# Attention scores from 64-row halves: one score product per head, a mask added by VectorE, and a new order of the steps

## The reference

```python
q, k = (rope(q), rope(k))
scores = jnp.einsum('bqhd,bkhd->bhqk', q, k) / math.sqrt(hd)
scores = jnp.where(causal, scores, jnp.asarray(-1000000000.0, scores.dtype))
probs = jax.nn.softmax(scores, axis=-1)
attn = jnp.einsum('bhqk,bkhd->bqhd', probs, v).reshape(Bb, Tt, d) @ Wproj
```

## Time and profile before

| | us |
|---|---|
| median of 3 runs | 1647.37 (1645.69 to 1647.99) |
| the profiled execution, own time | 1637.57 |
| its span, first to last instruction | 1635.7 |
| TensorE busy | 1437.9 (88%) |
| VectorE busy | 1033.1 (63%) |
| ScalarE busy | 912.9 (56%) |
| GpSimd busy | 717.7 (44%) |

### The profile page before, as it was taken

The page is one execution under the profiler, slowest core; times in us unless marked ns, Lnnn a source line. Parts: engine busy times, 40 slices in busy tenths (PEclk is TensorE's granted clock), DMA queues, the critical chain, the costliest instruction groups (busy, mean ns, idle before and its releaser), DMA issues.

```text
span 1635.7 us, 27557 instructions
## 1 busy us (share of the span) xinstructions
PE 1437.9 (88%) x9777; PEld 1248.5 (76%) x9777; DVE 1033.1 (63%) x2453; ACT 912.9 (56%) x2160; POOL 717.7 (44%) x712
## 2 busy tenths in 40 slices
PE   7988699999999997589869898889865999999996
PEld 5767599999999986466747666667654999999996
DVE  2998367766776757466756776768554555655552
ACT  5876255555555532267756676758744545554552
POOL 0787443344334114433453545644334444544443
PEclk9998799999999998799988998989876999999998
DMA  5410356555655531676575675676533223433312
GB/s 179 136 56 31 84 164 182 154 163 174 180 155 163 147 112 43 111 125 123 115 131 110 112 136 101 114 126 110 94 129 100 73 55 90 97 90 88 52 22 26
DMA packets 139448, 182.00 MB, mean 111 GB/s; under 512 B 22485, under 2 KB 107296, under 8 KB 139312
## 3 DMA queue, kind: packets, MB, share of 16 engines
q1 hardware_dynamic: 110512, 127.23, 31.3%
q0 software_dynamic: 28160, 51.96, 16.0%
q10 hardware_dynamic: 640, 1.05, 0.4%
HBM read 107.28 MB, written 42.08 MB: 91 GB/s over the span
## 4 chain that ended last, share of the span: by engine, by line
PE 67%; DVE 13%; issue 7%; another core or an unknown queue 7%; ACT 3%; POOL 2%; DMA 1%; SPq 1%; ACTq 0%; DVEq 0%; POOLq 0%
PE banks L942 41%; PE banks L1473 4%; PE banks L1430 4%; PE banks L451 3%; PE banks L1526 2%; PE banks L1004 2%; DVE hidden L977 2%; PE banks L1486 2%; PE banks L1447 1%; DVE lo_w L911 1%; DVE rm L1727 1%; DVE X L1695 1%; PE banks L1540 1%; DVE smax L1685 1%
## 5 line engine op out<-in xcount | busy, mean ns | idle before, releaser
L942 PE MATMUL banks<-hi_x,hi_w 128*128 128x320 f32 (+1 forms) x832 | 293.6, 353 | 35.0 <-DVE hidden L977 24.8
L942 PE MATMUL banks<-lo_x,hi_w 128*128 128x320 f32 (+1 forms) x832 | 288.5, 347 | 0.0
L942 PE MATMUL banks<-hi_x,lo_w 128*128 128x320 f32 (+1 forms) x832 | 288.2, 346 | 0.0
L942 PE MATMUL banks<-hi_w,hi_h 128*128 128x256 f32 x896 | 261.4, 292 | 5.9 <-issue 3.5
L884 POOL DMA_INDIRECT xe<-pooled,idx x160 | 155.5, 972 | 228.3 <-PE banks L1004 183.3
L942 PE MATMUL banks<-lo_w,hi_h 128*128 128x256 f32 x896 | 254.1, 284 | 0.0
L942 PE MATMUL banks<-hi_w,lo_h 128*128 128x256 f32 x896 | 254.0, 284 | 0.0
L942 PEld LDWEIGHTS banks<-hi_x,hi_w 128*128 128x128 f32 x832 | 160.2, 192 | 57.8 <-DVE hidden L977 29.7
L1878 POOL DMA_INDIRECT out<-X,tab x64 | 106.7, 1667 | 200.5 <-DVE X L1978 185.9
L1579 ACT ACTIVATE PN<-banks,smax 128x256 f32<-128x256 f32 (+1 forms) x512 | 180.2, 442 | 14.8 <-DVE smax L1685 13.8
L942 PEld LDWEIGHTS banks<-hi_w,hi_h 128*128 128x128 f32 x896 | 171.9, 192 | 7.6 <-issue 5.1
(11 more groups left out here) (186 smaller groups left out, 3101.0 us busy)
## 6 DMA issues: line engine op xcount, KB each, us to landing
w<-in_L_ffn_w SPq DMA_DIRECT2D x96, 256.0 KB, 5.6
done<-res SPq DMA_DIRECT2D x32, 640.0 KB
QS<-parts_qk SPq DMA_DIRECT2D x128, 128.0 KB
BIG<-in_L_ffn_W SPq DMA_DIRECT2D x16, 1024.0 KB
KS<-parts_qk SPq DMA_DIRECT2D x120, 128.0 KB
mask<-in_c_masks SPq DMA_DIRECT2D x16, 257.0 KB, 2.8
pooled<-XF SPq DMA_DIRECT2D x16, 256.0 KB, 3.3
WS<-in_L_cond_W SPq DMA_DIRECT2D x16, 256.0 KB
```

The source lines that it names most:

```text
L942: last = e.matmul(o, a[i], b[j], start=start and k == 0, stop=stop and k == 2, skip_group_check=True)
```

## The change

The block of zeros goes: `KS` keeps the two heads of a pair on rows 0 to 63 and 64 to 127, without the other halves, and GpSimd's memsets go. Scores are made for one head at a time, from 64 rows. Part 0 of a group is now the second query tile of all four heads: four products of 256 columns, head halves in turn, the halves in banks 0 and 1. Parts 1 and 2 are the first query tile of one half each: a mask product of 256 columns and two products of 128, both in bank 2; part 2 waits for part 1's semaphore. The mask of the second tile is no longer a product: VectorE adds it, while it takes the row minimum of the negated sum and writes that sum to `PN`, and ScalarE takes the exponentials there in place. The next group's part 0 waits for VectorE's row maxima instead of ScalarE's exponentials. The eight table entries of a routing group are issued four in each of two items. The five tables are new, and the number of instructions in a round differs only by these parts.

```diff
-    KS1 = sb("KS1", [P, HQ, NPAIR, T], F32R, place)
+    KS1 = sb("KS1", [P, NPAIR, T], F32R, place)
...
-    tri_q = np.where(p[None, :] > p[:, None], -1e9, 0.0)
+    tri_q = np.concatenate([np.zeros((P, P)), np.where(p[None, :] > p[:, None], -1e9, 0.0)], 1)
...
     PE_ROUND = (
-        ("rank", -3), ("scores", -1, 3, 0), ("turn_p", -1, 2, 2), ("scores", -1, 3, 1), ("values", -1, 1),
...
+        ("norm_turn", 1), ("scores", -1, 3, 1), ("turn_p", -1, 2, 2), ("turn_p", -1, 2, 0), ("scores", -1, 3, 2),
...
+    def entry_at(b, i):
+
+        if group_ended(b) is not None:
+            return group_ended(b), i
+        return (group_ended(b - 1), TB * K1 + i) if group_ended(b - 1) is not None else None
...
     def stack(e, b, x):
         e.wait_ge(s_qk_lo, 2 * b + x + 1)
-        if b < 2 and x == 1:
-            e.wait_ge(s_blocks, b + 1)
...
-                dst = KS[b % 2][rows_, s, :, :] if x else QS[b % 2][rows_, :, :]
+                dst = (KS if x else QS)[b % 2][rows_, :, :]
...
     def pe_scores(e, G, part):
-        if G >= 1:
-            e.wait_ge(s_pn, exp_count(G - 1, part))
-        if part < 2:
-            pair = 2 * g + part
-            e.matmul(PS[:, part, :].rearrange("p (h a k) -> p h a k", h=HQ, a=2)[:, :, 1, :], ident_b[:, :],
-                     wide(causal[:, :], 1, [P, HQ, P]), start=True, stop=False, skip_group_check=True)
-            last = e.matmul(PS[:, part, :], QS[b % 2][:, pair, P:T], KS[b % 2][:, :, pair, :],
-                            start=False, stop=True, skip_group_check=True)
+        half = lambda t, s: t[b % 2][s * P // HQ:(s + 1) * P // HQ]
+        if part == 0:
+
+            if G >= 1:
+                e.wait_ge(s_smax, 5 * (G - 1) + 4)
+            for x in range(2):
+                for s in range(HQ):
+                    last = e.matmul(PS[:, s, x * T:(x + 1) * T], half(QS, s)[:, 2 * g + x, P:T], half(KS, s)[:, 2 * g + x, :],
+                                    start=True, stop=True, skip_group_check=True)
+                    if x == 1:
+                        last.then_inc(s_s[s], 1)
         else:
-            e.matmul(PS[:, 2, :].rearrange("p (h k) -> p h k", h=HG), ident_b[:, :], wide(causal[:, :], 1, [P, HG, P]),
-                     start=True, stop=False, skip_group_check=True)
+
+            s = part - 1
+            if s == 1:
+                e.wait_ge(s_s[2], 2 * G + 1)
+            elif G >= 1:
+                e.wait_ge(s_pn, exp_count(G - 1, 2))
+            e.matmul(PS[:, 2, s * T:(s + 1) * T].rearrange("p (h k) -> p h k", h=2), ident_b[:, :],
+                     wide(causal[:, :], 1, [P, 2, P]), start=True, stop=False, skip_group_check=True)
             for x in range(2):
-                pair = 2 * g + x
-                last = e.matmul(PS[:, 2, x * T:(x + 1) * T], QS[b % 2][:, pair, 0:P], KS[b % 2][:, :, pair, 0:P],
-                                start=False, stop=True, skip_group_check=True)
-        last.then_inc(s_s[part], 1)
+                last = e.matmul(PS[:, 2, (2 * s + x) * P:(2 * s + x + 1) * P], half(QS, s)[:, 2 * g + x, 0:P],
+                                half(KS, s)[:, 2 * g + x, 0:P], start=False, stop=True, skip_group_check=True)
+            last.then_inc(s_s[2], 1)
...
             elif step == "row_max":
-                e.tensor_reduce(smax[:, G % NPN, col:col + heads_], PS[:, part, :].rearrange("p (x k) -> p x k", x=heads_),
-                                AX.X, ALU.max, negate=True).then_inc(s_smax, 1)
+                if part < 2:
+
+                    for x in range(2):
+                        cols, col = slice(x * T, (x + 1) * T), 2 * part + x
+                        e.tensor_tensor_reduce(PN[:, slot, part, cols], PS[:, part, cols], masks[:, :], -1.0, 3.0e38,
+                                               ALU.add, ALU.min, smax[:, slot, col:col + 1]).then_inc(s_smax, 1)
+                else:
+                    e.tensor_reduce(smax[:, slot, HG:2 * HG], PS[:, 2, :].rearrange("p (x k) -> p x k", x=HG),
+                                    AX.X, ALU.max, negate=True).then_inc(s_smax, 1)
```

More of the change, by code:

```diff
@@ L1177, in _build @@
[L1177 to L1180, removed]
-    DVE_ROUND = (
[L1182 to L1188, removed]
@@ new lines, in _build @@
+        ("qk", 1, 0), ("qk", 1, 1), ("values", -1, 1), ("turn_p", -1, 2, 1), ("gate_turn", -2),
+        ("turn_p", -1, 3, 2), ("turn_p", -1, 3, 0), ("values", -1, 2), ("rank", -3), ("turn_p", -1, 3, 1),
+        ("turn_qk", 1, 0), ("scores", 0, 0, 0), ("scores", 0, 0, 1), ("values", -1, 3), ("x_turn", 2),
+        ("scores", 0, 0, 2), ("gate", -2), ("scores", 0, 1, 0), ("outputs", -1, 0), ("turn_p", 0, 0, 2),
+        ("outputs", -1, 1), ("turn_p", 0, 0, 0), ("turn_qk", 1, 1), ("scores", 0, 1, 1), ("out_turn", -1),
@@ new lines, in _build @@
+        ("scores", 0, 1, 2), ("turn_p", 0, 0, 1), ("scores", 0, 2, 0), ("proj", -1), ("matrix", 2),
+        ("turn_p", 0, 1, 2), ("scores", 0, 2, 1), ("turn_p", 0, 1, 0), ("scores", 0, 2, 2), ("scores", 0, 3, 0),
+        ("values", 0, 0), ("turn_p", 0, 1, 1), ("v", 1))
+    DVE_ROUND = (
+        ("row_max", -1, 2, 0), ("row_max", -1, 2, 1), ("proj", -2), ("norm", -2, 1), ("matrix", 1),
+        ("norm", 1, 0), ("row_max", -1, 2, 2), ("route", -3, 1), ("scale", 1, 0), ("row_max", -1, 3, 0),
+        ("row_max", -1, 3, 1), ("combine", 2, 0), ("row_max", -1, 3, 2), ("scale", -2, 1), ("qk", 1, 0),
+        ("qk", 1, 1), ("route", -3, 2), ("route", -3, 3), ("combine", 2, 1), ("place", -3), ("row_max", 0, 0, 0),
+        ("split", 1, 0), ("row_max", 0, 0, 1), ("row_max", 0, 0, 2), ("gate", -2), ("row_max", 0, 1, 0),
+        ("outputs", -1, 0), ("outputs", -1, 1), ("row_max", 0, 1, 1), ("route_shift", -2), ("split", 1, 1),
+        ("row_max", 0, 1, 2))
@@ L1207, in _build @@
     PE_LAST = (
[L1208 removed]
+        ("turn_p", 15, 2, 2), ("scores", 15, 3, 1), ("values", 15, 1), ("turn_p", 15, 2, 0),
         ("turn_p", 15, 2, 1), ("gate_turn", 14), ("scores", 15, 3, 2), ("values", 15, 2), ("gate", 14),
@@ L1390, in pool_attn @@
         for step, b, d in rounds(POOL_FIRST, POOL_ROUND, POOL_LAST):
-            if step == "blocks" and b == 0:
-                e.memset(KS0[:, :, :, :].bitcast(F32), 0.0).then_inc(s_blocks, 1)
-            elif step == "blocks":
-                pool_zero_blocks(e)
-            elif step == "got":
+            if step == "got":
                 t, k = d
@@ L1413, in pool_attn @@
                                 ALU.add).then_inc(s_base, 1)
-            elif step == "entry" and group_ended(b) is not None:
-                g = group_ended(b)
-                t0 = r1.tiles(g)[0]
+            elif step == "entry" and entry_at(b, d[0]):
+                g, i = entry_at(b, d[0])
+                tt, k = r1.tiles(g)[0] + i // K1, i % K1
                 if d[0] == 0:
```

93 lines of the change are left out of this document (46 added, 47 removed).

## The result

| | before | after |
|---|---|---|
| median of 4 runs, us | 1646.53 | 1733.63 (1727.33 to 1739.09) |
| ratio | | 1.0532, interval 1.0491 to 1.0573 |
| span of the profiled execution, us | 1635.7 | 1725.5 |
| mean granted clock of the span | 0.934 | 0.907 |

It is 87 us slower. The forecast was 1681, slower by 34, in a range that ended at 1712. All but some 9 us of the difference of the two spans lies in the attention stage, between the first and the last addition of the residual: fifteen items took 483.6 us and now take 564.2. First the windows of the changed kernel, as in the earlier trace rows: the stage, an item without table entries, one with four, a late one.

What follows compares the result with a forecast made beforehand. TensorE's pace was taken to bound the attention stage, besides 67.6 us idle and a clock of 0.91. Scores add 34 us, all else 0: 1637.57 + 34 = 1671.6, plus 9.8 to the runs' median, 1681; range 1632 to 1712.

Steps and rivals of the forecast that it cites:

- Scores on TensorE, net 2.1 us an item, 34 us: Attention scores: changing to 64-row products and back costs TensorE 0.34 us each time, net 34 us for 16 items (27 to 56).
- An undisturbed item of 29.4: Attention stage: sign that the forecast is right, an item without stalls takes TensorE about 29.4 us instead of 27.3.
- Row maxima, exponentials, earlier release: 0: VectorE's masked maxima (1.2 us more an item, hidden by TensorE), ScalarE's in-place exponentials and earlier bank release: 0 each.
- The new wait of part 2 on part 1's signal: Rival, chance 0.11: in the first group TensorE waits for its own late signal, 33 us more, 1714.
- Entries: 0, with 38 us less as the bound: GpSimd's table entries, four in each of two items: taken as 0, at best every item 29.7 us, 38 us less.
- New tables otherwise: 0, because what they can win is idle time: New instruction order of the engines: 0, since its possible gain is idle time, which hangs on TensorE's late signals.
- The rival on tables: Rival, chance 0.20: the new order takes TensorE's waiting away, 74 us to win, three quarters of it giving 1626.
- The transfers that go with the late signals are the same: Argument against a gain from the new order: SP's transfers of stacked queries stay, so a stall remains in each item.
- The lower clock, left at 34 instead of 37: Extra score work on TensorE: 37 us at the granted clock of 0.91, kept at 34 as part falls into waiting.
- The 44 us that I had put down to the clock before: Attention stage before the change: the lower clock level holds about 18% of the time, half of that, 44 us, lost.

Runs made afterwards that it cites:

- r_rows: The kernel before with the scores of parts 0 and 1 made from 64 rows, part 2 still from 128; measured 1.0231 (1.0176 to 1.0286), 38 us slower.

## Why the prediction was right in one step and wrong in another

- *Scores on TensorE, net 2.1 us an item, 34 us.* Right: 1.93 of work an item, 33 us by the kernel with 128 rows. The halves run beside one another: a part 0 starts its products in pairs, at 907.70 and 907.71, then 907.92 and 907.93. In `r_rows`, where a part has two products of the same half, eight visits an item cost 38. The Trainium skill, "TensorEngine Tiling (Array Packing)", section Key Properties, has the mode switch drain the engine. The price agrees: 0.29 us more for each part in `r_rows`, 0.63 for 0.34.
- *An undisturbed item of 29.4.* Right: 29.1 without the indirect DMAs.
- *Row maxima, exponentials, earlier release: 0.* Not right, by the old order: the saving of the mask products was already in the term above, so that this term at 0 would have made the kernel with VectorE's mask 14 us faster. It is as fast as before (0.9997); the 10.1 us of work that it saves went into waiting and clock, 14.4. No run prices this term in the new order.
- *The new wait of part 2 on part 1's signal.* It did not decide. In the whole program TensorE's mask products waited 4.9 us for "remote". The wait is real, though: 10.6 us in the stage without the stack, 15.9 in that with 128 rows.
- *Entries: 0, with 38 us less as the bound.* Wrong in this order. Spread in the old order they gain 6; in the new order the scatters cost 39.6 us more in the profiled stages (72.4 - 32.8), idle time and clock about half each. I looked for a gain in them only.
- *"New tables otherwise: 0, because what they can win is idle time."* This is the step that failed. A table can lose idle time too, and I had not bounded it from that side. Without entries the new kernel has no more idle time than the old one (-0.2 us); with them the new order adds the 39.6 us above, and entries moved to another place of the same order give 34 back. With the parts of before the tables lose 63 us, a part of it in a wait that the changed kernel doesn't have. The rival on tables was worked out in the direction of a gain alone.
- *"The transfers that go with the late signals are the same."* This was the reason behind it, and it was a misreading: the earlier trace rows showed SP's transfers, which run at the same time; GpSimd's six gathers ran from 884.40 to 891.6 in the same stretch, and I did not put its timeline beside the others. Had I done so, the move of `entry` and `got` to the place of `outputs` would have been the first thing to price.
- *The lower clock, left at 34 instead of 37.* Wrong in size: 31.2 us more went to it. In an item with entries TensorE works in short pieces between late signals, and its granted clock is 0.79, where one of the items ahead of the entries has 0.90. The 44 us that I had put down to the clock before counted TensorE's idle time too; of its busy time 30.0 were lost.

Of 80.6 us in the stage, 28.9 are thus work, some 40 (30 by whole runs) are entries beside the new order, and most of the remaining 12 is clock that is lost without entries too. The 9 us ahead of the stage stay unexplained. They need not come from the change: in the kernel with the entries spread, whose first scatter comes only at 843.8, the stage starts 8 us later too (738.4 for 730.6).

## What to carry to other kernels

Before a wait marked "remote" is put down to something, lay the timelines of all engines that run in it side by side, and take as suspects all that run, not the first. Changes to an order on one engine are priced by what they then stand beside: the same 64 scatters on GpSimd cost 33 us of the stage in one order and 72 in the other, where they run beside a chain of short TensorE steps that wait for one another through other engines. And a new order has two signs: bound what it may lose as well as what it may win.

## What the runs showed of the hardware that was not expected

While GpSimd issues indirect DMAs one behind another (about 1 us each, 1.3 apart), more than half of TensorE's signals come over 1 us late (110 of 191 in the changed kernel's stage; half of the late ones by over 3.0 us, the latest by 11.0); VectorE's and ScalarE's don't, and without these DMAs none does. The Trainium skill, "Perfetto Trace Analysis", section Per-instruction lifecycle, says that a TensorE instruction's profiled window ends before its semaphore update is visible to the others. The trace agrees, 907.77 to 912.22 above. What joins the late signals to GpSimd's DMAs is not shown by any run here. That 64 rows of one half and 64 of the other cost 33 us in all, though their products overlap, is the price of changing the shape in nearly every score step, as the part of `r_rows` shows that went from 0.34 to 0.63.
